# Moving the zeroing of four result tables from one stage of a graph network to the next

## The reference, cut to what matters

```python
x = _layernorm(x + gat(x, edge_index, ...))        # softmax over a node's edges, skip map, elu
# second layer, for every edge e with nodes src[e], dst[e]
mid_s = concat([wA * es * sh0, wD * (ev . sh1) / sqrt(3)])
mid_v = concat([wB * es * sh1, wC * ev * sh0])
ns = segment_sum(mid_s, src, num_segments=N)       # the sums that the result tables hold
nv = segment_sum(mid_v, src, num_segments=N)
deg = segment_sum(ones, src, num_segments=N)
x = _layernorm(x + norm(linear(ns, nv, deg) + sc))
```

## Time and profile before

| | |
|---|---|
| median of 3 runs | 6377.99 us (6374.91 to 6380.39) |
| span of the profiled execution | 6385.1 us |
| what lies around its span | not shown; no further time of this execution is given |
| TensorE, VectorE, GpSimd, ScalarE busy | 93%, 86%, 74%, 59% of the span |
| moved by DMA | 1298 MB |

### The profile page before, as it was taken

One profiled execution on the slowest core, in us unless ns is written; L12 is line 12 of the kernel. 1 busy time (PEld: TensorE's weight loads), 2 busy tenths in 40 slices (PEclk: granted clock), 3 DMA queues, 4 the chain that ended last, 5 costly groups with the idle time before them and its releaser, 6 DMA issues.

```text
span 6385.1 us, 227589 instructions
## 1 busy us (share of the span) xinstructions
PE 5967.2 (93%) x48182; PEld 4370.4 (68%) x48183; DVE 5501.1 (86%) x17614; ACT 3747.7 (59%) x12831; POOL 4714.7 (74%) x4057
## 2 busy tenths in 40 slices
PE   6899999999999988899999999999999999999976
PEld 5555555555555555567777777777777777777754
DVE  2899999999999989988888888888888888888878
ACT  2566666666666654456666666666666666666622
POOL 2777777777777755557777777777777777777778
PEclk8999999999999988899999999999999999999999
DMA  5889998888898864479999999999999999999998
GB/s 192 227 263 263 263 264 263 263 263 264 264 264 263 263 206 152 154 149 165 166 166 165 166 165 166 166 166 165 166 166 165 166 166 166 166 166 166 165 284 293
DMA packets 1269305, 1298.01 MB, mean 203 GB/s; under 512 B 220815, under 2 KB 1180560, under 8 KB 1269168
## 3 DMA queue, kind: packets, MB, share of 16 engines
q0 software_dynamic: 328176, 468.28, 46.5%
q1 hardware_dynamic: 941090, 829.29, 42.2%
HBM read 695.18 MB, written 601.74 MB: 203 GB/s over the span
## 4 chain that ended last, share of the span: by engine, by line
PE 54%; issue 3%; DVE 3%; POOL 2%; DMA 0%; ACT 0%; DVEq 0%; POOLq 0%; SPq 0%; ACTq 0%
PE PS L973 12%; PE PS L952 11%; PE PS L941 11%; PE PS L989 9%; PE PS L1003 6%; PE PS L1000 2%; PE PS L911 1%; POOL d_n L603 1%; DVE arena L1274 1%; PE PS L961 1%; DVE arena L1266 1%; POOL out L597 0%; DVE stat L1282 0%; PE PS L919 0%; PE PS L960 0%
## 5 line engine op out<-in xcount | busy, mean ns | idle before, releaser
L585 POOL DMA_INDIRECT part<-arena,c_idx x1664 | 2585.6, 1554 | 759.1 <-issue 708.2
L546 POOL DMA_INDIRECT big<-h_tab,big x1664 | 1632.0, 981 | 512.0 <-PE PS L864 244.6
L864 PE MATMUL PS<-big 128*128 128x260 f32 x3328 | 952.9, 409 | 162.5 <-DVE big L1171 156.9
L660 ACT ACTIVATE big<-PS,arena 128x128 f32<-128x128 f32 x1664 | 513.6, 359 | 667.0 <-PE PS L854 667.0
L1179 DVE TENSOR_TENSOR big<-big,PS 128x260 f32 x1664 | 699.8, 421 | 210.1 <-PE PS L864 152.8
L952 PE MATMUL PS<-arena 128*128 128x256 f32 x3328 | 869.2, 384 | 1.6 <-DVE arena L1340 1.3
L973 PE MATMUL PS<-arena,w2m 64*64 64x128 f32 (+2 forms) x13312 | 859.2, 316 | 0.0
L864 PEld LDWEIGHTS PS<-big 128*128 128x128 f32 x3328 | 563.8, 189 | 422.1 <-issue 227.0
L1316 DVE TENSOR_TENSOR arena<-PS,arena 128x384 f32<-128x384 f32 x832 | 463.7, 557 | 426.3 <-PE PS L989 413.7
L941 PE MATMUL PS<-ident,arena 128*128 128x128 f32 x4992 | 728.6, 282 | 1.2 <-DVE arena L1350 1.2
L730 ACT COPY arena<-PS 128x384 f32<-128x384 f32 x1664 | 722.0, 491 | 3.2 <-PE PS L941 3.2
(11 more groups left out here) (182 smaller groups left out, 11630.3 us busy)
## 6 DMA issues: line engine op xcount, KB each, us to landing
w_tab<-big SPq DMA_DIRECT2D x416, 520.0 KB
arena<-w_tab SPq DMA_DIRECT2D x1664, 130.0 KB
part<-arena SPq DMA_DIRECT2D x1664, 32.1 KB
ot_tab<-big SPq DMA_DIRECT2D x416, 128.0 KB
arena<-ot_tab SPq DMA_DIRECT2D x416, 128.0 KB
arena<-src_tab SPq DMA_DIRECT2D x416, 128.0 KB
arena<-part SPq DMA_DIRECT2D x392, 128.5 KB, 3.5
big<-h_tab,big POOLq DMA_INDIRECT x1664
```

The costliest lines, as they stand in the source:

```text
L546: pool.indirect_dma_start(hg[:, s, k, :], None, h_tab, bass.IndirectOffsetOnAxis(ap=sidx[:, s, k:k + 1], axis=0)).then_inc(s_hg[s], 16)
L585: pool.indirect_dma_start(part[q], bass.IndirectOffsetOnAxis(ap=c_idx[:, s, k:k + 1], axis=0), o_cmb[:, s, k, :], None, compute_op=ALU.add ...
L864: mm(PS[:, 2 + k % 2, 0:HW], oh[:, p, k, :], hg[:, p, k, :], start=True, stop=True).then_inc(s_agg, 1)
```

## The change

The zeroing leaves attention's steps. The tables shrink to NP + 128 = 12,672 rows, 99 blocks of 128. In blend SyncE issues, behind the store of each step, four transfers, one for each table: block b of 128 rows x 1028 bytes is seen as 16 x 2 runs of 4112 bytes (four rows), and the source is 16 partitions of 4112 bytes, each read twice. A last block follows after the loop. The source is no longer a tile of its own, but rows 16 to 31 of `rows`, a tile of 33 partitions of which only rows 0 and 32 hold data; VectorE clears all of it at the start. SyncE's wait for `s_zero` is gone; GpSimd's stays, with the new count of 4 x 99.

```diff
-    ZERO = -(-(NP + P) // (NG * 32))
-    part = [dram(f"part{k}", [NG * 32 * ZERO, OR], F32) for k in range(GROUP)]
+    part = [dram(f"part{k}", [NP + P, OR], F32) for k in range(GROUP)]
...
         block_row, window_row = rows[0:1, :], rows[32:33, :]
+        ZERO = 4 * OR
+        zeros = rows[16:32, 0:ZERO].bitcast(F32)
...
-        zeros = cut(ZERO * OR)[0:32, :]
...
                 if there(g):
-                    for k in range(GROUP):
-                        sp.dma_start(part[k][ds(g * (32 * ZERO), 32 * ZERO), :].rearrange("(p r) d -> p (r d)", p=32),
-                                     zeros[:, :]).then_inc(s_zero, 16)
                     wait(sp, s_wev, 6 * (g - 3))
...
             sp.wait_ge(s_acc, GROUP * NG)
-            sp.wait_ge(s_zero, 16 * GROUP * NG)
+
+            def clear(b):
+                for k in range(GROUP):
+                    sp.dma_start(part[k][ds(b * P, P), :].rearrange("(p o r) d -> p o (r d)", p=16, o=2),
+                                 zeros.rearrange("p (o n) -> p o n", o=1).to_broadcast([16, 2, ZERO])
+                                 ).then_inc(s_zero, 16)
+
...
                     sp.dma_start(one(x1b, b - 3), b_x1[:, m, :]).then_inc(s_bst[m], 16)
+                if there(b):
+                    clear(b)
 
             steps(sp, NB, 3, 3, step_b)
+            clear(NB)
...
-            pool.wait_ge(s_zero, 16 * GROUP * NG)
+            pool.wait_ge(s_zero, 16 * GROUP * (NB + 1))
...
-            for tile in (zeros, fc2, two):
+            for tile in (rows, fc2, two):
                 v.memset(tile[:, :], 0.0)
```

## The result

The changed kernel takes 6677.12 us in the median (6674.91 to 6678.71, 4 runs), the kernel before 6379.19 us (6374.91 to 6385.85, 4 runs): a ratio of 1.0463, interval 1.0448 to 1.0478, 298 us more. The forecast was 6571, 193 us of loss, and its range ended at 6670. The direction and the place were right; the loss was half as large again. The prediction's own spread for the clears, a factor of 1.3, reached 6689 and held the measured time; its stated range was laid lower to take in the first rival.

A forecast was written before the change was run, and what follows sets the result against it. Attention was taken as bound by a TensorE-VectorE ring, and blend after the change by DMA: 6385.1 - 1 (attention) + 190 (blend) + 4 (last clear) = 6578 us of span, 6571 for the median, range 6376 to 6670.

The forecast's parts named there:

- the first rival: Blend: 16 partitions read at full speed, DMA hidden, SyncE's eight issues decide; 6389 us (6377 to 6401), chance 0.20.
- Attention, priced at nothing: Attention: the TensorE-VectorE ring keeps the 5.13 us step without zeroing; only the first steps gain, 0 to 3 us, 1 taken.
- The third rival: Attention: SyncE sets the step after all, which loses at most 0.37 us, 154 us in all; 6236 us, chance 0.05.
- the step most in doubt: Blend: the middle value, 4.1 us a block, for clears read from 16 partitions, between 1.32 and 12.5 us.
- The lower bound: Blend: a block's clears at the result stores' 25 GB/s an engine over 16 engines take 1.32 us.
- The addition of clears and loads: Blend: clears' 4.1 us plus other transfers' 2.07 us make 6.2 us of DMA a block, without overlap.
- the DMA engines then set the pace: Blend: 6.2 us of DMA a block against 4.26 makes the engines the limit; chance 0.68.
- The step that failed: Blend: a block takes just its 6.2 us of DMA, so 98 x (6.2 - 4.26) = 190 us more.
- SyncE's price: Blend: four added issues a block make 4.1 to 5.0 us of issuing, middle 4.5, hidden under the DMA.
- The hidden memset: Start: VectorE's larger clear, some 1.4 us, 1.2 more than before, is hidden by its 1.18 us idle for GpSimd's constants.
- the tail: After blend's loop: the last clear delays the next stage's first loads on the same queue by up to 4 us.
- the second rival: Blend: full-speed reads, but pauses let the clock fall, blocks of 5.5 us, 122 us more; 6499 us, chance 0.05.

The follow-up runs named there:

- spread32: Against the changed kernel: zeros read from 32 partitions, four apart over all 128, each once, still four clears a block; 6460.8 us, ratio 1.0122.
- act_one: Against one_transfer: its one clear a block issued by ScalarE, on a queue of its own; 6660.5 us, ratio 1.0436 to before.
- spread16: Against the changed kernel: the 16 source partitions lie eight apart, each still read twice, four clears a block; 6471.2 us (1 run).
- one_transfer: Against the changed kernel: one clear of 526 KB a block in place of four of 131 KB, same 16 neighbours; 6640.1 us, ratio 1.0402.
- issue_only: Against the kernel before, zeroing still in attention: four extra 8 KB transfers a block in blend, in 64-byte runs; 6475.8 us, ratio 1.0146.
- near32: Against the changed kernel: zeros read from 32 neighbouring partitions (64 to 95), each once, still four clears a block; 6448.7 us, ratio 1.0102.

## Why the prediction was right and wrong

- Attention, priced at nothing with 1 us at its start: right. Its step and its two waits are unchanged, and SyncE's new room there stays unused.
- The third rival (SyncE paces attention): out, by the same rows.
- 131.6 KB from 16 partitions as the step most in doubt, with 4.1 us a block for four of them: measured 4.3. The direction was argued; the size was the middle between bounds a factor of 9 apart, and that it came so near is luck. The lower bound fits another source: spread32 has 1.4. The small loads of the earlier trace rows give 17 GB/s an engine, 1.9 us for a block's clears; the 1.3 us that the prediction ascribes to them is the rate of the earlier trace rows. Neither carried over to a stream from 16 neighbours, 7.2 GB/s in act_one.
- The addition of clears and loads, 4.1 + 2.07 = 6.2: right as a sum of work, 6.36 us. The reason given, that packets on an engine do not overlap, does not follow from shares that add to 101%; that the addition holds, and for two queues too, act_one shows.
- That the DMA engines then set the pace: right in the main. SyncE's eight issues take 5.23 us a block where they set the pace (spread16), less than the 6.36 of DMA, and in the changed kernel SyncE stands at them (1.04 us for a load). Loads of xT are what GpSimd waits for, as the prediction wanted to see.
- **The step that failed** is the next: that a block then takes no longer than this work, 6.2 us, as if the 16 engines were full. The prediction asked for a DMA share above 0.9; it is 0.88, and 6.36 us of work take 7.25. 98 x 0.89 = 87 us of the 106 by which 6571 was passed are this idle time; 98 x 0.16 = 16 are the sum's own error.
- SyncE's price was said to be hidden under the DMA, and that failed in part. Three issues fewer (one_transfer) save 37 us: 0.49 us a block, of which 0.34 is less DMA work and only 0.15 less idle time. A cost that is alone 92 us, beside one that is alone 259 us, gave 298 and not the larger of the two: 39 us of it came on top. The price itself, 2.15 us for four issues and 4.5 us for a block, was too low: issue_only has 2.64 and 5.25. So the first rival was too cheap as well: spread32, nearly its full-speed source, takes 6461 us where it had 6389.
- The hidden memset (1.45 us at the start, and the next long instruction of VectorE 0.3 us later), the tail and GpSimd's wait: the first scatter comes 21 us after the convolution's first issue (3063.24 after 3041.84 us), 20 before. From the first issue of the convolution to the end the kernels take 3632 and 3631 us. The last clear's four issues take 3.96 us just ahead of that first issue, as much as the 4 us set down for it.
- The clock, the second rival: it did fall, to 0.51, and with the DMA engines setting the pace it cost nothing that shows. Whether it adds to the 80 us of spread32 (0.75) was not separated; SyncE without a wait in either stretch speaks for the issues.

Where the idle time lies, the DMA views of 2600 to 2640 us show, first the changed kernel, then issue_only (mean busy share of the 16 engines, in tenths, for each us):

```profile
DMA  8998798998977689797889879787979896699999
```

```profile
DMA  2792036951085711869211992037971088611799
```

In issue_only all engines stand still together between bursts; in the changed kernel no us of these 40 is under 0.6. Counted from the packets of its trace, fewer than 8 were in progress in only 9 of the 264 us from 2436 to 2700. So the 12% are some engines that stand idle while others work, and with one issue a block it is the same, 0.74 us while SyncE stands for 4 us at a load. What stays open is which engines these are and why: the packets are not recorded by engine.

## What to carry to other kernels

A transfer that is cheap by its bytes has three prices to be checked one by one: the engines' time at the rate of its own source, the issues in the queue it is moved to, and the loads that stand behind it. The engines' time, added up, is the least that a block can take when they set its pace; here a block took 14% more. When zeros, constants or any broadcast are read by DMA from few partitions, spread the source over all 128 (here 32 of them, four apart) and issue one large transfer; here that took a loss of 298 us to none. And before moving work off an engine that looks full, see whether anyone waits for it: SyncE was busy nearly all of attention's step, and freeing it gained less than 1 us.

## What the hardware showed unexpectedly

In these kernels the time of an issue went with the transfer's pattern, not with its bytes. Issues of a clear on SyncE (one line's instructions: duration in ns min/median/max), in the order near32 (32 rows side by side), spread32 (32 rows four apart) and the changed kernel (16 x 2):

```profile
L426 SPq DMA_DIRECT2D part<-rows x396: 351/375/1032, 2329.5 to 2813.0; - x198
```

```profile
L426 SPq DMA_DIRECT2D part<-rows x396: 468/543/602, 2329.3 to 2823.2; - x198
```

```profile
L426 SPq DMA_DIRECT2D part<-rows x396: 574/602/2242, 2330.1 to 3039.7; - x198
```

375, 543 and 602 ns in the median for the same 131,584 bytes; in one_transfer it is 603 for four times as many, in issue_only 588 for 8 KB. The issues from which the price was taken (L405 of the earlier trace rows, L483 of the earlier trace rows) were of the cheap kind, 381 ns in the median in both.
